# Thirty-two-bit exponentials always written to SBUF, and their low halves on DVE read from there instead of from PSUM

## What is computed

```python
x = x + _layernorm(_L0_attn_ref(_layernorm(x), wq, wk, wv, wo))
x = x + _layernorm(_L0_ffn_ref(_layernorm(x), ...))      # a mixture of 8 experts

# in _L0_attn_ref, per batch and head
q, k = apply_rotary_emb(q), apply_rotary_emb(k)
scores = einsum('bhid,bhjd->bhij', q, k) * HEAD_DIM ** -0.5     # causal
probs = softmax(scores)
out = einsum('bhij,bhjd->bhid', probs, v)
```

## Time and profile before

| | |
|---|---|
| median of 3 runs | 1211.6 us (1211.09 to 1211.76) |
| the profiled execution's own time | 1211.64 us |
| its span, first to last instruction | 1209.6 us |
| busy PE, DVE, ACT, POOL | 93%, 80%, 78%, 78% |
| attention's scores, first to last | 62.5 to 936.9 us of the span |

### The profile page before, as it was taken

How to read it: one execution, slowest core, us unless ns; L and a number is a source line. 1 busy time by engine, 2 the same in 40 slices (tenths; PEclk the granted TensorE clock), 3 DMA queues, 4 the chain that set the end, 5 groups by cost and what they waited for, 6 DMA issues and landing times. The chain is left out here.

```text
span 1209.6 us, 34888 instructions
## 1 busy us (share of the span) xinstructions
PE 1126.5 (93%) x13543; PEld 788.0 (65%) x13543; DVE 968.5 (80%) x2220; ACT 944.3 (78%) x2193; POOL 947.0 (78%) x984
## 2 busy tenths in 40 slices
PE   4689999999999999999999999999999598999996
PEld 1246777777777777777777777777777354566553
DVE  7799797887979787878879797978764559777987
ACT  3667988989797978889797979789899574766574
POOL 3478899999989999999989999999677474334463
PEclk9699999999999999999999999999999799999998
DMA  6652525253452515252543515253420200000011
GB/s 201 161 140 52 126 71 117 61 141 82 96 128 50 141 38 140 71 140 61 118 108 71 141 37 141 66 126 80 102 67 3 52 1 2 1 1 1 2 36 36
DMA packets 50660, 97.03 MB, mean 80 GB/s; under 512 B 6720, under 2 KB 23360, under 8 KB 48448
## 3 DMA queue, kind: packets, MB, share of 16 engines
q1 hardware_dynamic: 50496, 94.81, 31.6%
HBM read 58.47 MB, written 34.60 MB: 77 GB/s over the span
## 5 line engine op out<-in xcount | busy, mean ns | idle before, releaser
L827 POOL TENSOR_TENSOR Plo<-P,Phi 128x512 f16<-128x512 f32 (+3 forms) x640 | 537.5, 866 | 65.5 <-ACT P L516 62.1
L513 ACT ACTIVATE Phi<-psS 128x512 f16<-128x512 f32 (+3 forms) x768 | 393.8, 513 | 128.1 <-PE psS L368 83.3
L516 ACT ACTIVATE P<-psS 128x512 f32<-128x512 f32 (+3 forms) x640 | 316.2, 495 | 0.0
L392 PE MATMUL psO<-V,Plo 128*128 128x65 f16 x2304 | 288.6, 194 | 0.0
L388 PE MATMUL psO<-V,Phi 128*128 128x65 f16 x2304 | 287.3, 192 | 0.0
L390 PE MATMUL psO<-V,Phi 128*128 128x64 f16 x2304 | 286.4, 192 | 0.0
L365 PE MATMUL psS<-Q,K 128*128 128x512 f16 (+3 forms) x768 | 251.4, 327 | 9.6 <-DVE Plo L672 5.6
L388 PEld LDWEIGHTS psO<-V,Phi 128*128 128x128 f16 x2304 | 219.4, 98 | 56.3 <-issue 0.3
L368 PE MATMUL psS<-Q,K 65*128 65x512 f16 (+3 forms) x768 | 252.1, 328 | 0.0
L721 DVE TENSOR_REDUCE pmax<-psX 128x1 f32<-128x512 f32 x384 | 242.6, 682 | 0.8 <-PE psX L452 0.3
L390 PEld LDWEIGHTS psO<-V,Phi 128*128 128x128 f16 x2304 | 213.7, 96 | 30.9 <-issue 0.2
(11 more groups left out here) (200 smaller groups left out, 2159.0 us busy)
## 6 DMA issues: line engine op xcount, KB each, us to landing
K<-k_way SPq DMA_DIRECT2D x48, 512.0 KB, 7.0
k_way<-HL SPq DMA_DIRECT2D x64, 256.0 KB, 4.1
q_way<-HL SPq DMA_DIRECT2D x60, 256.0 KB, 3.7
Q<-q_way SPq DMA_DIRECT2D x60, 256.0 KB, 7.0
Q<-q_way SPq DMA_DIRECT2D x15, 512.0 KB, 11.8
out<-y SPq DMA_DIRECT2D x8, 256.0 KB, 2.2
y<-in_x SPq DMA_DIRECT2D x3, 512.0 KB, 11.2
hn<-in_x SPq DMA_DIRECT2D x3, 512.0 KB, 5.6
```

Of the source, the lines that this page charges most:

```text
L392: mm = nc.tensor.matmul(O, M.Plo[:, U % NP_, k * P:(k + 1) * P], V[:, HD:2 * HD + 1], start=False, stop=j == t, skip_group_check=True)
L513: nc.scalar.activation(M.Phi[:, U % NP_, 0:w], X, ACT.Exp, scale=SCALE)
L516: nc.scalar.activation(full, X, ACT.Exp, scale=SCALE).then_inc(S.exp_done, 1)
L827: nc.gpsimd.tensor_tensor(M.Plo[:, U % NP_, 0:w], M.P32[:, U % NP_, 0:w], M.Phi[:, U % NP_, 0:w], ALU.subtract).then_inc(S.lo_pool, 1)
```

## The change

The 32-bit exponential of every unit now goes to `P32` in SBUF. DVE's low halves read it there, so both of their inputs lie in SBUF; before, one lay in PSUM. PE's `scores(U + 3)` waits on `exp_done` for every unit. Nothing is added or removed, and no instruction changes its place on its engine. `P32` keeps its six buffers: ACT at unit U already waits for the low half of unit U - 6, for either engine.

```diff
@@ scores (PE)
                 if U >= NS:
-                    if lo_on_pool((U - NS) % SU):
-                        pe.wait_ge(S.exp_done, U - NS + 1)
-                    else:
-                        pe.wait_ge(S.lo_dve, COUNTS.dve[U - NS])
+                    pe.wait_ge(S.exp_done, U - NS + 1)
@@ exps (ACT)
-                full = M.P32[:, U % NP_, 0:w] if lo_on_pool(U % SU) else X
-                nc.scalar.activation(full, X, ACT.Exp, scale=SCALE).then_inc(S.exp_done, 1)
+                nc.scalar.activation(M.P32[:, U % NP_, 0:w], X, ACT.Exp, scale=SCALE).then_inc(S.exp_done, 1)
@@ low (DVE)
-                nc.vector.tensor_tensor(M.Plo[:, U % NP_, 0:w], M.psS[:, U % NS, 0:w], M.Phi[:, U % NP_, 0:w],
+                nc.vector.tensor_tensor(M.Plo[:, U % NP_, 0:w], M.P32[:, U % NP_, 0:w], M.Phi[:, U % NP_, 0:w],
                                         ALU.subtract).then_inc(S.lo_dve, 1)
```

## The result

The changed kernel takes 1237.11 us (median of 4 runs, 1233.15 to 1237.89) against 1211.34 us before (4 runs as well): a ratio of 1.0218, 95% interval 1.02 to 1.0237, +25.8 us. Forecast were +15 us and a range of 1212 to 1248. The profiled execution was the fastest of the four, so the profile shows 21.5 us of the loss (span 1231.1 against 1209.6 us).

The account below looks back on a forecast made before the run. PE sets the pace (54.33 of 54.40 us busy a steady slot), with POOL near the limit at 51.45. Costs of 14.3 and 5.2 less gains of 2.5 and 2.0 give +15 us: 1226.6 us from 1211.6, range 1212 to 1248.

Parts of the forecast that it names:

- The mechanism: Attention: DVE's two-SBUF-input low half and POOL's SBUF-reading instructions each wait for the other's whole instruction; as-forecast case, 1214 to 1240 us, 0.60.
- The price of one meeting: DVE low half against POOL instruction, 8 a slot: POOL loses 0.46 us, DVE waits 0.35 us, up to 2.8 a slot.
- The gains: PE's waits for DVE's low halves end earlier: -2.5 us over the 13 steady slots, -2 us in the last two.
- The cost on POOL: Steady slots: POOL loses 3.7 us to the lock, making PE 1.1 us late per slot, 14.3 us over 13.
- The walk: One steady slot followed: POOL's idle before L848 and L838 takes up 1.25 us; PE still comes 1.1 us late.
- The cost on DVE: Row maxima behind the waiting low half empty PE's side banks late: 0.4 us a steady slot, 5.2 us in all.
- Absorbed: Rival: POOL's idle time holds the lock if a meeting costs under 0.37 us; 1210 to 1214 us, chance 0.12.
- Its waits add up: Rival: POOL's idle time stays, DVE's lateness reaches PE through the side banks; 1240 to 1260 us, chance 0.18.
- A faster kernel: Rival: no lock for this pair of forms, only the earlier release stays; PE gains 9 us, 1203 us, chance 0.10.
- The signs announced: Trace signs: L672 about 1.0 us, POOL 50 to 60 us busier, PE's waits moving from L672 to POOL's L827.

Follow-up runs that it names:

- experiment 2: Changed kernel, but DVE's instruction for units 4 and 8 is a one-SBUF-input reduction, subtraction left out, early release kept: 1209.87 us, ratio 0.9981.
- experiment 3: As experiment 2 (one SBUF input on DVE), but PE waits again for DVE's low half: 1210.9 us, ratio 0.9991.
- experiment 1: Changed kernel, but PE's scores(U+3) waits again for DVE's low half of units 4 and 8: 1242.03 us, ratio 1.0252.
- experiment 8: Experiment 2's kernel plus a 120-column POOL instruction (POOL's filler) at each of DVE's 128 units: 1239.3 us, ratio 1.0195.
- experiment 11: Experiment 2's kernel plus a 304-column DVE instruction (the filler) ahead of each low half, the 128x8 copy written as a reduction: 1226.37 us, ratio 1.013.
- experiment 12: Experiment 2's kernel with both fillers, POOL's 120-column and DVE's 304-column instruction, the 128x8 copy written as a reduction: 1228.18 us, ratio 1.0144.
- experiment 5: Changed kernel with POOL relieved: from the second slot's rotated rows on, L848 makes half of its low halves: 1223.27 us, ratio 1.0101.
- experiment 9: Experiment 2's kernel plus a 304-column DVE instruction ahead of each of the 128 low halves, the 128x8 copy kept: 1236.76 us, ratio 1.0208.
- experiment 7: Changed kernel with DVE's low half as two subtractions of 256 columns, both with two SBUF inputs: 1311.16 us, ratio 1.0817.

## Why the prediction held, and which term was off

**The mechanism was right.** A DVE subtraction with two SBUF inputs and POOL's instructions, which read SBUF, exclude each other, whole instruction by whole instruction. The changed kernel and experiment 2, which differ in the second SBUF input and the subtraction alone, lie 27 us apart.

**The price of one meeting was right on POOL and a little low on DVE.** POOL: 0.46 us forecast, 3.4 / 8 = 0.43 in a steady slot. DVE: 0.35 forecast, 1117 - 688 = 429 ns measured, and 4.1 us of busy time a slot against 2.8. The forecast took half of POOL's mean instruction. But an instruction that arrives at any time meets a long one more often than a short one. With each of POOL's instructions in the slot 790.8 to 845.2 weighed by its length, and POOL's idle time counted as no wait, the mean wait is 0.56 us, and less the 0.14 under the start it is 0.42: an estimate, from the durations in the trace of before.

**The gains were near.** For the last two slots -2 us, measured -1.3 (from 49.8 and 41.9 to 49.7 and 40.7 us). For the steady slots I kept -2.5; experiments 2 and 3 show nothing there without the lock, and experiment 1 shows some 5 us there with it.

**The two loss terms were mis-sized, in opposite directions.** "The cost on POOL", 14.3 us, was followed through the slot as if DVE were on time. By itself POOL's loss costs about 0.3 us a slot (experiment 8's first six steady slots), some 4 us over 13, and beside DVE's lateness nothing more (experiments 11 and 12). The walk also used up the idle time before L838 as cover, and that stayed. "The cost on DVE" had 5.2 us, because I took most of DVE's 9.1 idle us as cover. The filler gives 15 us over the 13 slots, for a DVE that loses 3 us a slot and not the 4 of the changed kernel. The runs line up: a steady slot's DVE busy time grew by 3.0, 3.1, 3.8, 4.1 and 10.1 us (experiments 11, 5, 9, the change, experiment 7), and the slot by 1.0, 1.1, 1.9, 1.7 and 8.0. Some 2 us of lateness are hidden, the rest goes to PE. My reading of it, which no run tests by itself: idle time of DVE that is spent in front of its low half, waiting for ACT, covers nothing that stands behind it.

The two errors partly cancel in the sum. That the two terms together (19.5 us) came near the 22 us that slots 1 to 13 lost is luck, and the sum of +15 is still 11 us short of the measured +25.8; only the range held it.

**What stays open.** The run with both fillers reaches 55.4 us a slot, the changed kernel 56.1; over slots 1 to 13 that is 728.0 against 737.4 us, so no run explains the last 9.4 us. DVE loses 4.1 us in the changed kernel's slot and 3.0 in the fillers': the copy, 0.48 us instead of 0.165, makes 0.3 of that, and the low halves, spread from 0.69 to 1.53 in one slot, the rest. By the line above, 1.1 us more of DVE's lateness is enough for the 0.7. A part by POOL is not excluded: PE's weight loads wait 11.6 us for POOL's low halves in the changed kernel, and 1.1 us in experiment 12. No run tells the two apart.

**The rivals.** "Absorbed" had its turning point at 0.37 us of POOL's time per meeting; it was 0.43, and POOL was not the engine to ask first. "Its waits add up" named the way through the side banks, which was the larger one, and that POOL's idle time stays because DVE is late too, which it did before L834; its size of 1240 us and more was not reached. A faster kernel shows only without the second input, in a kernel that leaves out a subtraction, and then by 2 us.

**The signs announced.** L668 at about 1.0 us: 1.117. POOL's busy time up 50 to 60 us: 45. A steady slot of 55.5 with POOL at 55: 56.1 and 54.8. Waits at L365 gone, new ones at L388 (now L385) for POOL: so, but not most at steps 33 to 39: of the 11.6 us only 1.6 lie at step 38, and 10.0 at steps 41 to 43. Slots 14 and 15 hardly changed: so.

## What to carry to other kernels

Before an operand of a DVE instruction moves from PSUM to SBUF, count its SBUF inputs. Here a second one made a subtraction of 688 ns take 1117 in the mean beside a POOL that is busy for 95% of the slot, and cost POOL about as much, though the same form undisturbed takes 683 ns. Look in the trace of before for a tiny DVE instruction with two SBUF inputs that takes a microsecond beside POOL: here L666, 24 elements and 1.17 us. And ask of idle time whether it lies behind the late instruction and ahead of the next engine's need; idle time in front of it, or one that the late engine itself ends, did not serve as cover here.

## What the runs showed that I had not expected

A DVE copy from SBUF to SBUF, 128x8, can wait much longer than a subtraction with two SBUF inputs. In experiment 8 it took 4.53 us, through six POOL instructions back to back: the last of the three at 509.56 and the five that follow it. Of the 99 subtractions that were held in the changed kernel, 98 got in at the first end of a POOL instruction. The copy doesn't always wait so long: in seven steady slots of the same run the copy took at most 0.45 us, and in the changed kernel up to 0.479, behind one POOL instruction. What decides between the two, no run shows. Written as a reduction it took 0.16 us beside the same POOL, and the run with both fillers went from 1263.66 to 1228.18 us for one instruction a slot. The Trainium skill (SBUF — State Buffer, "Who interferes with whom") names copies among the instructions that can take the shared pair; this case agrees, with 4.53 us beside POOL against 0.165 in the kernel before.

Halving an instruction that takes this lock cost 74 us (1237 to 1311), since more than half of the halves wait anew.
